# A two-layer graph network on one core: an unread matmul added to each step of layer 1, and bounded register loads

## The reference

```python
def layer0(h, edge_bias, src, dst, Wq, Wk, Wv, Wp, bp, ...):
    Q, K, V = h @ Wq, h @ Wk, h @ Wv                 # per head
    score = einsum('ehd,ehd->eh', K[src], Q[dst]) / sqrt(HD) + edge_bias
    ex = exp(score - segment_max(score, dst)[dst])
    attn = ex / segment_sum(ex, dst)[dst]
    out = segment_sum(attn[:, :, None] * V[src], dst) @ Wp + bp
    h1 = layer_norm(h + out)
    return layer_norm(h1 + gelu(h1 @ W1 + b1) @ W2 + b2)

def layer1(h, src, dst, W_lin, b_lin, W_gat, attn_l, attn_r, gat_bias):
    h = h @ W_lin + b_lin
    feat = h @ W_gat                                  # per head
    el, er = sum(feat * attn_l), sum(feat * attn_r)
    e = leaky_relu(el[src] + er[dst], 0.2)
    a = softmax of e over the edges of each dst
    return h + leaky_relu(segment_sum(feat[src] * a, dst) + gat_bias, 0.01)

x = x + layer0(relu(layernorm(x)), ...)
x = x + layer1(relu(layernorm(x)), ...)
```

## Time and profile before

| | |
|---|---|
| median of 3 runs | 6279.49 us (6277.37 to 6281.22) |
| span of the profiled execution | 7245.2 us |
| edge phase of layer 0 in it | about 430 to 3240 us |
| phase of nodes | about 3240 to 4233 us |
| edge phase of layer 1 | about 4293 to 6995 us |

### The profile page before, as it was taken

How to read it: one execution, slowest core, us unless ns; L and a number is a source line. 1 busy time by engine, 2 the same in 40 slices (tenths; PEclk the granted TensorE clock), 3 DMA queues, 4 the chain that set the end, 5 groups by cost and what they waited for, 6 DMA issues and landing times.

```text
span 7245.2 us, 120511 instructions
## 1 busy us (share of the span) xinstructions
PE 5958.1 (82%) x26094; PEld 4610.4 (64%) x26094; DVE 4961.3 (68%) x12464; ACT 3156.2 (44%) x10275; POOL 3702.4 (51%) x4022
## 2 busy tenths in 40 slices
PE   8967778777788778778999948888878887878888
PEld 5546556555566566557999946666666666666666
DVE  4568888778788888886777736666666656666664
ACT  3345445444445444443333324444444444444433
POOL 1155555555555555533444455655665656566523
PEclk9989999999998989999999966666666666666679
DMA  5667777777777777763222236666666666666647
GB/s 180 201 211 232 240 225 237 223 231 228 222 235 227 231 223 230 226 193 93 85 84 84 84 107 167 169 166 168 168 165 168 168 163 168 166 171 170 166 144 232
DMA packets 722973, 1313.16 MB, mean 181 GB/s; under 512 B 109087, under 2 KB 502131, under 8 KB 722420
## 3 DMA queue, kind: packets, MB, share of 16 engines
q0 software_dynamic: 200192, 634.41, 32.5%
q1 hardware_dynamic: 444802, 422.18, 20.0%
q10 hardware_dynamic: 77426, 250.73, 8.9%
HBM read 964.16 MB, written 342.73 MB: 180 GB/s over the span
## 4 chain that ended last, share of the span: by engine, by line
PE 43%; DVE 19%; issue 17%; another core or an unknown queue 11%; ACT 5%; DVEq 2%; POOL 1%; ACTq 0%; DMA 0%; SPq 0%; POOLq 0%
PE bank L813 38%; DVE ev L1280 4%; DVE sred L1195 4%; PE bank L816 4%; DVE prod L1189 3%; DVE acc L1295 3%; ACT absd L618 2%; DVEq L1177 1%; POOL Gf L573 1%; DVE U L1247 1%; ACT oh L623 1%; DVE Y L1248 1%; DVE scan L1257 1%; DVE scan L1237 1%
## 5 line engine op out<-in xcount | busy, mean ns | idle before, releaser
L813 PE MATMUL bank<-ev,oh 128*128 128x264 f32 x7040 | 2546.3, 496 | 197.4 <-DVE ev L1280 149.5
L522 POOL DMA_INDIRECT Gf<-kv_tab,srcs x1564 | 1499.1, 958 | 1356.2 <-DVE ev L1280 830.2
L522 POOL DMA_INDIRECT Gf<-ft_tab,srcs x1564 | 1624.5, 1039 | 1085.7 <-DVE ev L1280 573.9
L813 PEld LDWEIGHTS bank<-ev,oh 128*128 128x128 f32 x7040 | 1606.1, 243 | 518.7 <-DVE ev L1280 191.3
L813 PE MATMUL bank<-qs,oht 128*128 128x256 f32 x3520 | 1039.4, 421 | 402.4 <-issue 199.1
L813 PE MATMUL bank<-Gf 128*128 128x128 f32 (+3 forms) x6480 | 1262.2, 346 | 23.7 <-ACT Gf L802 18.4
L1280 DVE TENSOR_TENSOR ev<-Gf,ex 128x528 f32<-128x528 f32 x1760 | 1230.3, 699 | 2.8 <-ACT ex L685 1.4
L1295 DVE SCALAR_TENSOR_TENSOR acc<-acc,same,bank 128x264 f32<-128x264 f32 x1540 | 737.8, 479 | 572.6 <-PE bank L813 280.5
L618 ACT ACTIVATE absd<-lane,dlocs 128x128 f32<-128x128 f32 x3520 | 1112.6, 389 | 4.1 <-DVE bms L1162 3.7
L813 PEld LDWEIGHTS bank<-Gf 128*128 128x128 f32 x6480 | 965.5, 191 | 223.1 <-issue 98.3
L813 PEld LDWEIGHTS bank<-qs,oht 128*128 128x128 f32 x3520 | 649.6, 205 | 635.0 <-issue 560.5
(11 more groups left out here) (160 smaller groups left out, 6243.3 us busy)
## 6 DMA issues: line engine op xcount, KB each, us to landing
sums<-acc ACTq DMA_DIRECT2D x440, 528.0 KB
qs<-q_tab SPq DMA_DIRECT2D x880, 128.0 KB
qs<-dst_tab SPq DMA_DIRECT2D x880, 128.0 KB
Gf<-sums SPq DMA_DIRECT2D x196, 132.0 KB, 2.2
kv_tab<-Gf SPq DMA_DIRECT2D x98, 260.0 KB, 2.1
Gf<-in_x SPq DMA_DIRECT2D x196, 128.0 KB, 2.2
Gf<-kv_tab,srcs POOLq DMA_INDIRECT x1564
Gf<-ft_tab,srcs POOLq DMA_INDIRECT x1564
```

Source lines behind the costliest of these rows:

```text
L522: pool.indirect_dma_start(out=rows[layer][:, m % SLOTS[layer], k, :], out_offset=None, in_=tab, in_offset=bass.IndirectOffsetOnAxis(ap=src ...
L813: return nc.tensor.matmul(o, a, r, start=first, stop=end)
```

## The change

In layer 1's edge phase, in every one of the 880 steps, PE does one more product between the spread and the aggregation: the identity as stationary operand, 256 columns of `w_l` as the moving one, into bank 0, without a wait and without a semaphore. Nothing reads the result. Besides, the loads of the registers that are waited on keep their runtime check of the bounds, on SP (`spans_of`, both layers, 8 values a block) and on POOL (the slot's count, both layers, 8 values for 8 spans); the fourth such load, `span_rows`, and DVE's `slots` stay as they are.

```diff
@@ spans_of, on SP
                 return nc.values_load_multi_w_load_instructions(
                     ready_rows[layer][:, b * ST:(b + 1) * ST], engines=[mybir.EngineType.SP], min_val=base + 1,
-                    max_val=base + NSPAN + 1,
-                    skip_runtime_bounds_check_because="a step's span is one of the spans or the one after them")[1]
+                    max_val=base + NSPAN + 1)[1]
@@ gathers, on POOL
                                 free = nc.values_load_multi_w_load_instructions(
                                     free_row[0:1, old:min(old + ST, NSPAN)], engines=[mybir.EngineType.Pool],
-                                    min_val=layer * NS + 1, max_val=layer * NS + NS,
-                                    skip_runtime_bounds_check_because="a span's last step is one of the NS steps")[1]
+                                    min_val=layer * NS + 1, max_val=layer * NS + NS)[1]
@@ on PE
+            def unread():
+
+                mm(bank[0][:, 0:D], ident[:, :], w_l[:, 0, :])
+
@@ edge_phase, on PE
                         C, r = step_at(B, s + 2)
                         if C.live:
                             spread(layer, C, r)
+                        if layer == 1 and B.live:
+                            unread()
                         C, r = step_at(B, s - 12)
                         if C.live:
                             agg(C, r)
```

## The result

The changed kernel takes 6112.16 us (median of 4, 6107.51 to 6115.96) where the kernel before takes 6279.88 (4 runs, 6277.37 to 6281.22): a ratio of 0.9737 with a 95% interval from 0.9724 to 0.975, 168 us less. The forecast was 5917 us, 362 us less: the direction is right, the time lies in the range, and the gain is less than half of what was forecast.

A forecast was written before the change was run, and what follows sets the result against it. PE at its lower clock was taken to bound layer 1. Blocks going from 24.8 to 21.0 us, 110 times, save 418 us, scaled by 0.867 to 362: 6279 - 362 = 5917 us, range 5720 to 6170 us.

The forecast's parts named there:

- the sum had 24.8 and 21.0: Layer 1's block of 8 steps: 24.8 us before, 20.7 + 0.3 = 21.0 us after the change.
- the forecast's 0.90: PE's clock in layer 1 after the change, taken between 0.65 as now and layer 0's 0.92.
- The comparison with layer 0 by the width of the records: PE steps: layer 0 has eight wide records at clock 0.92, layer 1 four wide and four narrow; the change makes six wide.
- The first rival's rule: PE's clock falls with idleness, so it stays at 0.65 and the kernel is slower, 6440 to 6880 us; chance 0.09.
- the signs given in advance: Trace of after: 1760 more records, layer 1 clock 0.85 or more, blocks 20 to 22 us, DVE's 232.0 us wait under half.
- the 0.47 of the sum: Added product on PE in layer 1: 0.47 us a step at the high clock, hidden in PE's idle time.
- I scale the gain alike: 418 x 0.867: Layer 1's 418 us gain on the profiled span, scaled by timed median over span to 362 us.
- POOL ... starts a gather every 0.95 + 0.30 = 1.25 us: POOL in layer 1, all slots free: two gathers for each of 782 spans make 1955 us, 17.8 us a block.
- What is late next: After the change, DVE: its own 17.7 us plus 2.1 us of boundary waits, 19.8 us a block, POOL right behind.
- The 0.3 us a block that I added for POOL: POOL's bounds checks in layer 1: between 0 and 1.2 us a block, a quarter of it added.
- The second one: Layer 1's clock rises to 0.80 but POOL's checks and DVE leave little gain: 6130 to 6290 us; chance 0.08.
- The third: Layer 1 at the short block's 19.2 us throughout, clock about 1.00, POOL's checks hidden: under 5745 us; chance 0.06.

The follow-up runs named there:

- The half gathers: Changed kernel, with and without the product, leaving out one of a span's two gathers in layer 1: 5873.84 us with, 6257.93 us without, in the short condition.
- the widths 8 to 512: Changed kernel with the product at 8, 128, 256 or 512 columns: short condition 6989, 6112, 6104 us, 512 not seen; long 7656, 7397, 7355, 7500 us.
- the 8 columns: Changed kernel with the added product at 8 columns in place of 256: 6989 us, ratio 1.114 in the short condition; 7656 us, 1.060 in the long.
- the checks alone: Changed kernel without the added product, only the bounds checks: 6276.13 us, ratio 1.000 in the short condition; 7327.83 us, 1.0136 in the long.
- the one run where they come in bursts: Changed kernel with the product at 128 columns and POOL waiting once for eight spans in layer 1: 8168.92 us, ratio 1.1291, in the long condition.

## Why the prediction was right or wrong

**What bounds the kernel before: right in the short condition.** PE at its lower clock is the bound of layer 1 there. The half gathers show it (0.2% of the time for half of POOL's work without the product, 384 us for the product then), and the clock of 0.71 means that 58% of the time is cold. In the long condition, from which the prediction's rows are, it was only part of the bound: the clock rose from 0.65 to 0.83, and a block took 25.2 and then 25.5 us where the sum had 24.8 and 21.0.

**The clock: right, and understated.** 0.98 in the short condition for the forecast's 0.90 (0.83 in the long one). The comparison with layer 0 by the width of the records was the step that carried it, and the widths 8 to 512 bear it out in order. The first rival's rule, that idleness alone lowers the clock, is refuted by the 8 columns. Of the signs given in advance these came true: 27854 - 26094 = 1760 more records, DVE's wait for PE before its add at 61.6 us for 232.0. A block took 18.9 us, not 20 to 22.

**The product's price while warm: right.** Two records of 256 columns are hidden in PE's idle time; in after they take 4803.09 - 4802.57 = 0.52 us, for the 0.47 of the sum, and PE waits before the next spread all the same:

```profile
4802.14 0.58 PE L811 MATMUL bank<-erq,oht 128*128 128x8 f32 x4 [1.71 <-DVE sred L1215]
4802.57 0.68 PE L811 MATMUL bank<-steps,ident 128*128 128x256 f32 x2
4803.09 1.07 PE L811 MATMUL bank<-ev,oh 128*128 128x264 f32 x4
4804.00 0.27 PE L814 MATMUL bank<-ident,S 128*128 128x128 f32 x1
4805.51 0.58 PE L811 MATMUL bank<-erq,oht 128*128 128x8 f32 x4 [1.25 <-DVE sred L1215]
```

**The step that failed: "I scale the gain alike: 418 x 0.867".** The 966 us between the span and the timed median weren't spread alike. In the short condition layer 0 took 0.846 of its length in the profile of before (2377 for 2810 us), the phase of nodes 1.00, and a block of layer 1 took 20.4/24.8 = 0.82. By the factor, a block was to go from 21.5 us to 18.2, 3.3 us; it went from 20.4 to 18.9, 1.5 us. Of the 1.8 us too much, 1.1 are in the block before. The marks of the long condition count its stops in, so a wait for nothing that the profile shows (205.9 us of `issue` before DVE's add, 149.8 of `remote` before its scan) was no property of this kernel. In the short condition DVE's waits in layer 1 of the checks alone are these:

```profile
DVE acc L1293 <- PE bank L811: 355.2, 358, 1.5
DVE sred L1209 <- issue: 86.1, 100, 1.3
DVE df L1263 <- PE bank L814: 82.9, 61, 1.7
```

355.2 + 82.9 = 438 us of DVE's waits end with PE, 4.0 us a block, and none is longer than 1.7 us. That is a bound on what a faster PE can give here, and 3.5 us a block of it came where POOL wasn't in the way. It lies above the 362 us forecast, so it wouldn't have lowered the forecast by itself: the floor had to be right as well.

**The second step that failed: "POOL ... starts a gather every 0.95 + 0.30 = 1.25 us", 17.8 us a block.** It is the other 0.7 us. The forecast pace, scaled to 18.2, was set against a POOL term that is too small and doesn't scale. After, POOL's waits in layer 1 are these, and no one is over 0.3 us:

```profile
POOL Gf L520 <- issue: 409.2, 1343, 0.3
POOL Gf L520 <- DMA Gf<-ft_tab,srcs: 39.3, 129, 0.3
POOL Gf L520 <- DVE ev L1284: 21.6, 71, 0.3
```

It is busy or issuing for 1581 + 470 = 2051 of 2057 us. The 1.25 us from start to start of rows 11 is that of one gather at the start of the phase; in the middle of layer 1 some take longer:

```profile
4801.27 0.95 POOL L520 DMA_INDIRECT Gf<-ft_tab,srcs  x1 [0.30 <-issue]
4802.53 1.24 POOL L520 DMA_INDIRECT Gf<-ft_tab,srcs  x1 [0.30 <-issue]
4804.07 0.94 POOL L520 DMA_INDIRECT Gf<-ft_tab,srcs  x1 [0.30 <-issue]
```

On average it is 18.9/14.2 = 1.33 us a gather (1564 of them in 110 blocks), and that is the 18.9 us a block. The trace of before has the same, in layer 1 (4293 to 6995 us):

```profile
L522 POOL DMA_INDIRECT Gf<-ft_tab,srcs x1517 | 1579.8, 1041 | 1064.8 <-DVE ev L1280 573.9 <-issue 490.9
```

A gather takes 1041 ns there on average, not 0.95 us. 1.04 + 0.30 = 1.34 us, times 14.2, is 19.0 us a block: the floor could have been read before the change ran, from the mean of the stage in place of one row.

What lengthens them can be read from the starts of both engines in after. Of the 242 gathers that began in the first 0.29 us of a weighing by DVE (L1284, both of its inputs in SBUF), 235 took over 1.15 us; of the other 1304, 26 did. With the checks alone in the short condition it was 367 of 367, and 12 of the other 1182. The 1.24 us above is such a one: the weighing began at 4802.26. No run moves the one against the other, so that the weighing holds the gather up is read from the times of these two traces alone.

DVE then waits for rows that POOL hasn't brought: 314.0 us before L1215 with SP's `landed` as the releaser. What is late next, which the prediction gave to DVE with POOL right behind, is POOL. With half of the gathers a block takes 16.9 us, so DVE's own pace is at most that, where I had 17.7; what bounds it at 16.9 isn't separated (PE is busy for 1791.53 of 1833 us there, DVE for 1630.19).

**The checks: right in the short condition, at nothing.** 0 was one end of the range and the measured ratio is 1.000. The 0.3 us a block that I added for POOL wasn't there: no wait of POOL in layer 1 of after is over 0.3 us, so its sequencer makes the checks while gathers run.

**The rivals.** The second one had the reason for the small gain in it (POOL within a few us of the pace), but tied it to a clock of 0.80 and to POOL's checks; it came with the clock at 0.98 and the checks at nothing. The third had the clock, about 1.00, and the hidden checks, and not POOL's floor.

**Luck.** That 6112 us lies in the range owes something to two errors that went opposite ways. With the measured clock the same sum would have been 0.96/19.2 + 0.04/30.4, 19.5 us a block, and about 5800 us, further from the result than 5917.

## What to carry to other kernels

Before a sum is made on a profile, hold its span against the timed runs; when they differ by 15%, one factor for all stages is a guess (here they took 0.85, 1.00 and 0.82 of their length), and the bound of the gain is to be taken from waits that a named engine ends, not from those of `issue` or `remote`. A matrix engine that is never idle can still be at half its clock: look at how wide its products are before more work is given to it, since wide unread work raised the clock here and narrow work lowered it. And when one engine's time is bought back, the next engine's free pace should be taken from its mean in the stage where it competes (1041 ns here), not from one instruction where it runs alone (0.95 us); leaving out half of its work then shows in one run whether it is the bound.

## What the runs showed of the hardware

- A PE busy for 2932.13 of 2933.00 us at a granted clock of 0.50 throughout, with products of 8 and 264 columns in turn; with 256 columns in place of the added 8 the clock is 0.98.
- A gather that POOL starts in the first 0.29 us of a DVE multiply with both inputs in SBUF takes over 1.15 us (235 of 242 in layer 1 of after, 26 of the 1304 others); the first of layer 1 in before takes 0.95 us.
- The same program takes 6277 or some 7200 us. In the long condition engines stop for some us with everything ready (4.8 us in the piece shown), DVE for up to 17.3 us with gathers in bursts, and single register instructions take up to 1393 ns in place of 18; the trace holds under half as many semaphore events of layer 1. The stops shrink where the gathers are halved, and were longer in the one run where they come in bursts. What they come from stays open.
- In the long condition more instructions cost where they are free in the short one: the bounds checks 1.4% against 0.0%, and the change as a whole is 2.8% slower there and 2.7% faster here. What such a change is worth holds for a condition, not for the kernel alone.
